# Gated feed-forward block on one core: the first of seven block products copied into the second's PSUM pair, and the second product moved behind that copy

## The chip, the core and the metric

The kernel runs on one core of a Trainium2 chip. The metric is device time in microseconds (us) of one execution; the kernel before has a median of 394.66 us over three runs (394.34 to 394.94). Engine names here: TensorE (PE in the rows), its weight loads (PEld), VectorE (DVE), ScalarE (ACT), GpSimd (POOL), and SP, which issues DMAs. SBUF is the on-chip memory of the engines, PSUM the accumulators that TensorE writes: eight banks, used here as four pairs `pair0` to `pair3` of 128 x 1024 float32.

## The reference

Four batches of 512 rows with 512 columns pass a gated cross-attention block and then a gated feed-forward block with ternary weights. Only the second part is touched:

```python
def ternary_quant(w):
    scale = jnp.mean(jnp.abs(w)) + EPS
    return jnp.clip(jnp.round(w / scale), -1.0, 1.0) * scale
...
x = x + jnp.tanh(g_xattn[0]) * xattn(layernorm(x), ctx_1024, Wq, bq, Wk, bk)
xn = layernorm(x)
hidden = jax.nn.silu(xn @ wu.T) * (xn @ wg.T)        # (4, 512, 512) x (2048, 512)
x = x + jnp.tanh(g_ffn[0]) * (hidden @ wd.T)         # (4, 512, 2048) x (512, 2048)
```

## The kernel before, in words

**Attention (0 to 92 us of the profile).** It is left as it is.

**Up and gate products, units 0 to 15.** A unit `n` makes a block of `hidden` for 256 of the 2048 expert columns and half of the 2048 rows; units 0 to 7 take the first half, 8 to 15 the second. The product is a 2 x 2 block product in seven block products (Winograd's form of Strassen's scheme). Activations are split into a high and a low float16 part, so one block product is 8 matmuls of 512 columns: up and gate (two banks of a PSUM pair), two inner chunks, high and low (`product`, L924 and L926). The seven are numbered 1 to 7 and accumulate in PSUM where the scheme allows it (`start=False`): 1, 6, 7 and 4 run on `ps_c[n % 2]` (`pair0` or `pair3`, by turns), 5 and 3 on `ps_z` (`pair2`), and 2 alone on `ps_y` (`pair1`).

The four result blocks are called by their place. ScalarE copies partial sums out between the products and VectorE adds the rest:

- "11" = product 1 + product 2: `copy_1` (ScalarE, L1373) copies `ps_c` after product 1 to SBUF, `add_11` (VectorE, L1789) adds `ps_y` to that.
- "12": `copy_u2` (L1383) copies `ps_c` after product 6, `add_12` (L1794) adds `ps_z`.
- "22": `copy_5` (L1395) copies `ps_z` after product 5, `add_22` (L1799) adds `ps_c` after product 7; product 4 waits for it.
- "21" = `ps_c` after product 4, read in place.

Each block then passes `silu` (ScalarE, L1344), `make_h` (VectorE, L1804: silu times gate) and the split into high and low parts (`high_h` on ScalarE, L1357, `low_h` on VectorE, L1809). Product 1 of unit n+2 overwrites the pair that `make_h(n, "21")` reads.

**Down product.** Units 0 to 5 go through it as plain matmuls, in `down_half(n)` within units 3 to 8 (32 matmuls of 512 columns, L1000). The rest is a second seven-product scheme, `final(g, j, t, ...)` (L1052, 256 columns), whose pieces 1, 5, 6, 3, 7, 2, 4 are strewn between the block products of units 9 and 10 (`between_two`, two tiles at once, 8 matmuls) and 12 to 15 (`between`, one tile, 8 matmuls). Their results lie in the `ps_c` pair that the unit itself does not use; VectorE adds them to the output (`final_evict`, L1855), and product 1 of the next unit (10, 11, 13, 14, 15) waits for the last of these seven additions, the one of piece 4 (`s_ef`), because it overwrites that pair. Each piece also waits for an earlier piece's addition where both use the same bank.

**Side work.** In units 0 to 7 ScalarE also rounds and signs the ternary weights of later units and of the down matrix (`round_unit` L1209, `sign_unit` L1215, `round_down` L1410, `sign_down` L1418). From unit 6 on GpSimd forms sums S1 to S4 of the result blocks for the second scheme, and ScalarE and VectorE split them (`high_s` L1363, `low_s` L1814).

Each engine's order is written out by hand in its own block; only semaphores tie them. On TensorE the order before is, for units 0 to 7, 6, 3, (`down_half`), 7, then 1, 2, 5 of the next unit, then 4. The lines that the change touches:

```python
            def product2(n):
                if n == 0:
                    pe.wait_ge(s_exp, NG)
                else:
                    pe.wait_ge(s_c["11"], n)
                product(n, 2, ps_y, A12, "B21", True)
...
                act.activation(cb(n, "11"), ps_c[n % 2][:, :], ACT.Copy).then_inc(s_cp1, 1)
...
                dve.tensor_tensor(cb(n, "11"), ps_y[:, :], cb(n, "11"), ALU.add).then_inc(s_c["11"], 1)
```

Of the kernel before, what the change touches and what calls it, by code (L numbers as in the profile page):

```python
# [6 lines left out]
def gated_block_kernel(nc, x, xT, first, ctxT, wqkT, wugT, wdT, x1_dram, out):  # L7
# [25 lines left out]
    NN = 2 * NU  # L33
# [12 lines left out]
    with stack:  # L46
# [55 lines left out]
        cbuf = {"11": [xf[:, 0:1024]], "12": [xf[:, 1024:2048]],  # L102
# [39 lines left out]
        s_c = {c: sem(f"s_c{c}") for c in ("11", "12", "22")}  # L142
# [624 lines left out]
        def _(pe):  # L767
# [265 lines left out]
            product2(G0 + 1)  # L1033
            product4(G0)
            product5(G0 + 1)
# [66 lines left out]
            product2(n + 1)  # L1102
            product4(n)
            product1(n + 1)
            product5(n + 1)
            for n in range(G1, NN):
# [8 lines left out]
                else:  # L1115
                    product2(n)
# [3 lines left out]
                    between(n, 5)  # L1120
                    product6(n)
# [17 lines left out]
            pe.wait_ge(s_c["11"], NN)  # L1139
# [27 lines left out]
        def _(act):  # L1167
# [163 lines left out]
            def silu(n, c):  # L1331
                if c == "21":
# [5 lines left out]
                    src = ps_c[n % 2][:, 0:512]  # L1338
                else:
# [80 lines left out]
            sign_part(2, 0)  # L1420
            act.wait_ge(s_t4, 1)
            copy_1(0)
# [4 lines left out]
            copy_u2(0)  # L1427
            silu(0, "11")
            for n in range(G0 + 1):
                down = n >= 3  # L1430
                if n > 0:
                    silu(n - 1, "21")
                    copy_u2(n)
# [4 lines left out]
                if n > 0:  # L1438
                    high_h(n - 1, "21")
# [62 lines left out]
                copy_1(n + 1)  # L1502
# [5 lines left out]
                if n == 1:  # L1508
                    copy_5(n + 1)
                    silu(n + 1, "11")  # L1510
                else:
                    silu(n + 1, "11")
                    copy_5(n + 1)
            for n in (G0 + 1, G0 + 2):
# [7 lines left out]
                else:  # L1522
                    high_s(n - 1, "S1")
                    high_h(n - 1, "21")
                    high_s(n - 1, "S2")
                    copy_5(n)
                    copy_1(n)
# [638 lines left out]
```

## Time and profile before

| what | value |
|---|---|
| median of 3 runs | 394.66 us (394.34 to 394.94) |
| span of the profiled execution, first to last instruction | 393.2 us |
| TensorE busy | 388.2 us, 99% of the span |
| VectorE busy | 330.2 us, 84% |
| ScalarE busy | 269.8 us, 69% |
| GpSimd busy | 183.9 us, 47% |
| `add_11`, 16 times | 19.5 us of VectorE |
| `copy_1`, 16 times | 16.2 us of ScalarE |

The profiled execution is one of its own; of it the page gives the span, and what lies around the span is not in it. The median of the runs is 1.46 us above that span. Matmuls are pipelined: a row's duration (0.38 us for 512 columns) is longer than the distance to the next start (0.21 to 0.22 us), and the ends are modelled, so a wait of TensorE shows as idle time only beyond that overlap of some 0.16 us.

### The profile page before, as it was taken

How to read it: one execution, taken by the hardware profiler on the slowest of the kernel's cores; microseconds unless marked ns; L12 is line 12 of the kernel's file. 1: busy time of each engine (PE TensorE's matmuls, PEld its weight loads, DVE VectorE, ACT ScalarE, POOL GpSimd, SP SyncE). 2: the span in 40 equal slices, each digit the busy share in tenths (PEclk: the TensorE clock that was granted, in tenths of full speed). 3: DMA queues.
4: the chain of work that ended last, by engine and by line, in shares of the span. 5: the costliest groups of instructions: out<-in, count | busy, mean ns of one | idle time of the engine just before them, and what ended most of it. 6: DMA issues, size and time to landing. Idle time of an engine off the chain costs nothing.

```text
span 393.2 us, 6214 instructions
## 1 busy us (share of the span) xinstructions
PE 388.2 (99%) x2000; PEld 219.3 (56%) x2000; DVE 330.2 (84%) x501; ACT 269.8 (69%) x366; POOL 183.9 (47%) x199
## 2 busy tenths in 40 slices
PE   8999999999999999999999999999999999999997
PEld 6676775554444444444444444556545665656886
DVE  0778897988799975789888979999999989798974
ACT  3887988899777786869897982856287566564400
POOL 0498727767845031403169462643639447261000
DMA  8999977799600030020029470006230000000014
GB/s 287 404 402 407 408 232 184 176 261 183 160 2 0 1 108 0 13 96 0 2 60 190 86 148 2 0 1 214 78 139 0 2 1 2 0 2 1 2 61 154
DMA packets 44048, 43.91 MB, mean 112 GB/s; under 512 B 30833, under 2 KB 33009, under 8 KB 42993
## 3 DMA queue, kind: packets, MB, share of 16 engines
q1 hardware_dynamic: 44016, 43.53, 36.3%
q8 instruction: 16, 0.26, 0.3%
q14 instruction: 16, 0.12, 0.1%
HBM read 29.89 MB, written 6.29 MB: 92 GB/s over the span
## 4 chain that ended last, share of the span: by engine, by line
PE 84%; DVE 6%; ACT 4%; issue 4%; DMA 1%; POOL 1%; DVEq 0%; ACTq 0%; POOLq 0%
PE pair L924 20%; PE pair L926 20%; PE pair L1052 14%; PE pair L1000 8%; PE pair L815 7%; PE pair L838 6%; PE pair L788 4%; PE pair L772 3%; PE pair L799 2%; DVE x_sb L1855 1%; DVE xf L1804 1%; DMA xf<-in_first 1%; PE pair L853 1%; DVE sh L1814 1%; ACT xf L1395 1%
## 5 line engine op out<-in xcount | busy, mean ns | idle before, releaser
L924 PE MATMUL pair<-xb_hi,w_sb 128*128 128x512 f16 x448 | 169.8, 379 | 0.9 <-DVE xf L1799 0.5
L926 PE MATMUL pair<-xb_lo,w_sb 128*128 128x512 f16 x448 | 169.8, 379 | 0.0
L924 PEld LDWEIGHTS pair<-xb_hi,w_sb 128*128 128x128 fp8e4 x448 | 43.8, 98 | 54.0 <-DVE xf L1799 1.3
L926 PEld LDWEIGHTS pair<-xb_lo,w_sb 128*128 128x128 fp8e4 x448 | 43.8, 98 | 49.5 <-issue 0.3
L1344 ACT ACTIVATE xf<-xf,small 128x512 f32<-128x512 f32 x48 | 34.5, 720 | 43.5 <-DVE xf L1799 23.6
L1804 DVE SCALAR_TENSOR_TENSOR xf<-xf,small 128x512 f32<-128x512 f32 x48 | 41.7, 870 | 8.5 <-ACT xf L1344 8.4
L1855 DVE SCALAR_TENSOR_TENSOR x_sb<-pair,small,x_sb 128x256 f32<-128x256 f32 (+1 forms) x85 | 37.4, 472 | 6.3 <-PE pair L1052 5.8
L1000 PE MATMUL pair<-x_sb,sh 128*128 128x512 bf16 x192 | 42.4, 379 | 0.0
L626 POOL TENSOR_TENSOR w_sb<-w_sb 128x512 fp8e4<-128x512 fp8e4 x8 | 8.8, 1101 | 55.1 <-ACT w_sb L1215 55.1
L1000 PEld LDWEIGHTS pair<-x_sb,sh 128*128 128x128 f16 x192 | 18.8, 98 | 22.6 <-DVE x_sb L1839 0.2
L1809 DVE TENSOR_TENSOR sh<-xf,sh 128x512 f16<-128x512 f32 x34 | 30.6, 906 | 0.9 <-ACT sh L1357 0.8
L1357 ACT ACTIVATE sh<-xf 128x512 f16<-128x512 f32 x34 | 20.9, 623 | 13.0 <-DVE xf L1804 12.3
L815 PE MATMUL pair<-sh,xt_sb 128*128 128x512 f32 (+2 forms) x80 | 28.6, 509 | 0.0
L1794 DVE TENSOR_TENSOR xf<-pair,xf 128x1024 f32<-128x1024 f32 x16 | 19.5, 1221 | 5.5 <-PE pair L926 5.4
L1789 DVE TENSOR_TENSOR xf<-pair,xf 128x1024 f32<-128x1024 f32 x16 | 19.5, 1220 | 3.8 <-issue 2.2
L713 POOL TENSOR_TENSOR xf<-xf 128x512 f32<-128x512 f32 x7 | 9.6, 1369 | 27.9 <-DVE xf L1804 27.9
L1373 ACT ACTIVATE xf<-pair 128x1024 f32<-128x1024 f32 x16 | 16.2, 1014 | 8.9 <-PE pair L926 6.4
L1799 DVE TENSOR_TENSOR xf<-pair,xf 128x1024 f32<-128x1024 f32 x16 | 19.5, 1218 | 2.3 <-PE pair L926 2.3
L1839 DVE SCALAR_TENSOR_TENSOR x_sb<-pair,small,x_sb 128x512 f32<-128x512 f32 x24 | 17.7, 745 | 3.9 <-PE pair L1000 3.9
L815 PEld LDWEIGHTS pair<-sh,xt_sb 128*128 128x128 f32 x80 | 13.9, 190 | 12.6 <-issue 10.5
L1383 ACT ACTIVATE xf<-pair 128x1024 f32<-128x1024 f32 x16 | 16.3, 1020 | 5.5 <-PE pair L926 5.3
L1209 ACT ACTIVATE w_sb<-w_sb,small 128x1024 f32<-128x1024 f32 x16 | 18.9, 1228 | 0.0
(207 smaller groups left out, 769.2 us busy)
## 6 DMA issues: line engine op xcount, KB each, us to landing
w_sb<-in_wugT SPq DMA_DIRECT2D x8, 1024.0 KB, 14.9
x_sb<-in_x SPq DMA_DIRECT2D x4, 1024.0 KB, 12.8
xf<-in_wdT SPq DMA_DIRECT2D x4, 1024.0 KB, 7.5
xt_sb<-in_wdT SPq DMA_DIRECT2D x4, 1024.0 KB, 4.9
xt_sb<-in_xT SPq DMA_DIRECT2D x12, 256.0 KB, 5.8
x_dram<-x_sb SPq DMA_DIRECT2D x8, 256.0 KB, 3.5
out<-x_sb SPq DMA_DIRECT2D x8, 256.0 KB, 4.2
x_sb<-x_dram SPq DMA_DIRECT2D x4, 512.0 KB, 3.9
```

The source lines that it names most:

```text
L815: last = pe.matmul(ps_x[i % 2][:, lo:hi], xt_tile(b, i)[:, k, :], at[:, k, lo:hi], start=(k == 0), stop=(k == KD - 1))
L838: last = pe.matmul(mix_bank(j)[:, i * 256:(i + 1) * 256], left[:, i, k * P:(k + 1) * P], right[:, k, :], start=j in (1, 5, 2) and i == 0 a ...
L924: pe.matmul(dst[:, m * 512:(m + 1) * 512], w[:, o:o + P], hi[:, k], start=start and k == 0, stop=False, skip_group_check=not start)
L926: last = pe.matmul(dst[:, m * 512:(m + 1) * 512], w[:, o:o + P], lo[:, k], start=False, stop=k == 1, skip_group_check=not start)
L1000: ins = pe.matmul(dst, h_part(n, c, lo)[:, i * P:(i + 1) * P], t_d[:, e * DM + lo_col:e * DM + hi_col], start=first and n == units[0] and ...
L1052: ins = pe.matmul(fin_bank(g, j, t), hidden(u, c, lo, min(t, NT - 1)), cols, start=first and u == units[0] and lo == 0 and not (side and t ...
L1344: act.activation(cb(n, c)[:, 0:512], src, ACT.Silu, scale=su[:, :]).then_inc(s_silu[c], 1)
L1357: act.activation(part(n, c, 0), shaped(n, c, cb(n, c)[:, 0:512]), ACT.Copy).then_inc(s_hi[c], 1)
L1789: dve.tensor_tensor(cb(n, "11"), ps_y[:, :], cb(n, "11"), ALU.add).then_inc(s_c["11"], 1)
L1804: dve.scalar_tensor_tensor(cb(n, c)[:, 0:512], cb(n, c)[:, 0:512], kap[:, :], gate, ALU.mult, ALU.mult).then_inc(s_mul[c], 1)
L1809: dve.tensor_tensor(part(n, c, 1), shaped(n, c, cb(n, c)[:, 0:512]), part(n, c, 0), ALU.subtract)\
L1855: dve.scalar_tensor_tensor(fin_rows(g, j, t), fin_bank(g, j, t), c_out[:, :], fin_rows(g, j, t), ALU.mult, ALU.add).then_inc(s_ef, 1)
```

## The change: what it does

`copy_1` writes into `ps_y` instead of SBUF. Product 2 now waits for that copy (`s_cp1`) and accumulates onto it (`start=False`), so "11" is complete in PSUM. `add_11` is gone. `silu(n, "11")` reads `ps_y` and writes SBUF, `make_h(n, "11")` takes its gate from `ps_y`, and `copy_1` waits until the unit before has passed that `make_h` (`s_mul["11"]`), since it overwrites `ps_y`. The orders on the three engines are rewritten. The core of the diff:

```diff
-                if n == 0:
-                    pe.wait_ge(s_exp, NG)
-                else:
-                    pe.wait_ge(s_c["11"], n)
-                product(n, 2, ps_y, A12, "B21", True)
+                pe.wait_ge(s_cp1, n + 1)
+                product(n, 2, ps_y, A12, "B21", False)
...
                 product1(n + 1)
+                product5(n + 1)
                 product2(n + 1)
-                product5(n + 1)
                 product4(n)
...
-            product2(G0 + 1)
+            product5(G0 + 1)
             product4(G0)
-            product5(G0 + 1)
             product1(G0 + 1)
...
                 between_two(n, 1)
                 between_two(n, 5)
+                product2(n)
                 product6(n)
...
                 between_two(n, 2)
-                product4(n)
-                between_two(n, 4)
-                product2(n + 1)
                 if n == G0 + 1:
+                    product4(n)
+                    between_two(n, 4)
                     product5(n + 1)
                     product1(n + 1)
                 else:
+                    between_two(n, 4)
+                    product5(n + 1)
                     product1(n + 1)
-                    product5(n + 1)
+                    product4(n)
+                    product2(n + 1)
...
-                    product2(n)
                     product5(n)
                     product1(n)
                     between(n, 1)
                     between(n, 5)
+                    product2(n)
                     product6(n)
...
+                elif c == "11":
+                    act.wait_ge(s_p[2], n + 1)
+                    if n == 0:
+                        act.wait_ge(s_tl, t_done(0, "T2"))
+                    else:
+                        act.wait_ge(s_lo["11"], n)
+                    if n > GB:
+                        act.wait_ge(s_sh["S3"], n - GB)
+                    src = ps_y[:, 0:512]
...
             def copy_1(n):
                 act.wait_ge(s_p[1], n + 1)
                 if n == 0:
-                    act.wait_ge(s_tl, t_done(0, "T2"))
-                else:
-                    act.wait_ge(s_lo["11"], n)
-                if n > GB:
-                    act.wait_ge(s_sh["S3"], n - GB)
-                act.activation(cb(n, "11"), ps_c[n % 2][:, :], ACT.Copy).then_inc(s_cp1, 1)
+                    act.wait_ge(s_exp, NG)
+                else:
+                    act.wait_ge(s_mul["11"], n)
+                act.activation(ps_y[:, :], ps_c[n % 2][:, :], ACT.Copy).then_inc(s_cp1, 1)
...
-            def add_11(n):
-                dve.wait_ge(s_p[2], n + 1)
-                hold(dve, s_cp1, n + 1)
-                dve.tensor_tensor(cb(n, "11"), ps_y[:, :], cb(n, "11"), ALU.add).then_inc(s_c["11"], 1)
...
-                gate = ps_c[n % 2][:, 512:1024] if c == "21" else cb(n, c)[:, 512:1024]
+                gate = {"21": ps_c[n % 2], "11": ps_y}.get(c, cb(n, c))[:, 512:1024]
```

In the rows below, a row with `pair1` as its output on TensorE is product 2, `pair2` product 5 or 3, `pair0` and `pair3` products 1, 6, 7, 4; the words in brackets are the semaphores waited for.

ScalarE between units 0 and 1, before: two weight roundings, `silu(0, "22")`, `copy_1(1)`, two splits, `silu(1, "11")`, `copy_5(1)`.

```order
L1209 ACTIVATE w_sb<-w_sb,small 128x1024 [waits s_inv]
L1209 ACTIVATE w_sb<-w_sb,small 128x1024
L1344 ACTIVATE xf<-xf,small 128x512 [waits s_coef,s_c22]
L1373 ACTIVATE xf<-pair3 128x1024 [waits s_lo11,s_p1]
L1357 ACTIVATE sh<-xf 128x512 [waits s_mul12]
L1357 ACTIVATE sh<-xf 128x512 [waits s_mul22]
L1344 ACTIVATE xf<-xf,small 128x512 [waits s_c11]
L1395 ACTIVATE xf<-pair2 128x1024 [waits s_tl,s_p5]
```

ScalarE in the same place now:

```order
L1208 ACTIVATE w_sb<-w_sb,small 128x1024 [waits s_inv]
L1208 ACTIVATE w_sb<-w_sb,small 128x1024
L1379 ACTIVATE pair1<-pair3 128x1024 [waits s_mul11,s_p1]
L1352 ACTIVATE xf<-xf,small 128x512 [waits s_coef,s_c22]
L1401 ACTIVATE xf<-pair2 128x1024 [waits s_tl,s_p5]
L1365 ACTIVATE sh<-xf 128x512 [waits s_mul12]
L1365 ACTIVATE sh<-xf 128x512 [waits s_mul22]
L1352 ACTIVATE xf<-pair1,small 128x512 [waits s_lo11,s_p2]
```

`copy_1` moved ahead of `silu(0, "22")` but stays behind the two roundings; `copy_5` moved ahead of the two splits.

TensorE at the end of unit 12, before: the last piece 4, product 2 of unit 13 (8 rows), then product 5; product 1 follows after 8 rows of product 5.

```order
L1052 MATMUL pair3<-w_sb,sh 128x256 [waits s_tw,s_lo22,s_ef]
L1052 MATMUL pair3<-w_sb,sh 128x256 x7
L924 MATMUL pair1<-xb_hi,w_sb 128x512 [waits s_c11]
L926 MATMUL pair1<-xb_lo,w_sb 128x512
L924 MATMUL pair1<-xb_hi,w_sb 128x512
L926 MATMUL pair1<-xb_lo,w_sb 128x512
L924 MATMUL pair1<-xb_hi,w_sb 128x512
L926 MATMUL pair1<-xb_lo,w_sb 128x512
L924 MATMUL pair1<-xb_hi,w_sb 128x512
L926 MATMUL pair1<-xb_lo,w_sb 128x512
L924 MATMUL pair2<-xb_hi,w_sb 128x512 [waits s_c12]
```

TensorE in the same place now:

```order
L1048 MATMUL pair3<-w_sb,sh 128x256 [waits s_tw,s_lo22,s_ef]
L1048 MATMUL pair3<-w_sb,sh 128x256 x7
L924 MATMUL pair2<-xb_hi,w_sb 128x512 [waits s_c12]
L926 MATMUL pair2<-xb_lo,w_sb 128x512
L924 MATMUL pair2<-xb_hi,w_sb 128x512
L926 MATMUL pair2<-xb_lo,w_sb 128x512
L924 MATMUL pair2<-xb_hi,w_sb 128x512
L926 MATMUL pair2<-xb_lo,w_sb 128x512
L924 MATMUL pair2<-xb_hi,w_sb 128x512
L926 MATMUL pair2<-xb_lo,w_sb 128x512
L924 MATMUL pair3<-xb_hi,w_sb 128x512 [waits s_ef,s_ev,s_mul21]
```

Between piece 4 and product 1 (the row that waits for `s_ef`) stood two products; now one stands there. The eight matmuls of product 2 come after the next pieces 1 and 5. The same holds in units 9, 10, 14 and 15.

VectorE at the start of unit 13, now: the addition of piece 4 of unit 12, three splits, two additions of pieces, `make_h(13, "11")` with its gate from `pair1`, `add_12`. Before, `add_11` (`L1789 TENSOR_TENSOR xf<-pair1,xf 128x1024`) stood behind the three splits.

```order
L1800 SCALAR_TENSOR_TENSOR c21<-c21,small,pair3 128x512 [waits s_silu21]
L1851 SCALAR_TENSOR_TENSOR x_sb<-pair0,small,x_sb 128x256 [waits s_fin]
L1810 TENSOR_TENSOR w_sb<-xf,w_sb 128x512 [waits s_shiS1]
L1805 TENSOR_TENSOR w_sb<-c21,w_sb 128x512 [waits s_hi21]
L1810 TENSOR_TENSOR w_sb<-xf,w_sb 128x512 [waits s_shiS2]
L1851 SCALAR_TENSOR_TENSOR x_sb<-pair3,small,x_sb 128x256 [waits s_fin,s_shift] x2
L1800 SCALAR_TENSOR_TENSOR xf<-xf,small,pair1 128x512 [waits s_silu11]
L1790 TENSOR_TENSOR xf<-pair2,xf 128x1024 [waits s_p3,s_cu2]
```

The addition of piece 4 is where it was; what was taken out stood behind it.

## Rows read from the trace of the kernel before

**Rows 1.** Stretches: time, busy time of PE, PEld, DVE, ACT, POOL, clock, DMA

```profile
92.00:230.00 138.00, 138.00 (x640) 62.29 (x639) 116.22 (x139) 110.76 (x128) 62.85 (x55) 1.00 0.27 66
230.00:300.00 70.00, 68.81 (x372) 35.62 (x370) 65.57 (x91) 41.10 (x62) 35.47 (x24) 1.00 0.23 71
300.00:366.00 66.00, 66.00 (x419) 40.72 (x418) 58.00 (x77) 39.33 (x59) 31.03 (x21) 1.00 0.00 1
```

**Rows 2.** Costliest groups of the page: the removed addition (busy, mean ns, idle before)

```profile
L1789 DVE TENSOR_TENSOR xf<-pair,xf 128x1024 f32<-128x1024 f32 x16 | 19.5, 1220 | 3.8 <-issue 2.2
```

**Rows 3.** Timeline, unit 10 (start, duration, engine): additions of piece 7; product 4, piece 4

```profile
278.32 0.86 DVE L1855 SCALAR_TENSOR_TENSOR x_sb<-pair,small,x_sb 128x256 f32<-128x256 f32 x2
...
277.84 0.38 PE L924 MATMUL pair<-xb_hi,w_sb 128*128 128x512 f16 x1
...
279.57 1.04 PE L1052 MATMUL pair<-w_sb,sh 128*128 128x256 bf16 x8
```

**Rows 4.** Timeline, unit 9: end of product 1, make_h(8,"21"), piece 1

```profile
247.45 0.75 DVE L1804 SCALAR_TENSOR_TENSOR c<-c,small,pair 128x512 f32<-128x512 f32 x1 [0.28 <-ACT c L1344]
...
247.69 0.38 PE L926 MATMUL pair<-xb_lo,w_sb 128*128 128x512 f16 x1
248.26 1.05 PE L1052 MATMUL pair<-x_sb,sh 128*128 128x256 bf16 x8 [0.18 <-DVE c L1804]
```

**Rows 5.** Timeline, units 9 and 10: add_22(9), additions of piece 4; products 4, 1

```profile
258.11 1.21 DVE L1799 TENSOR_TENSOR xf<-pair,xf 128x1024 f32<-128x1024 f32 x1
...
264.56 0.86 DVE L1855 SCALAR_TENSOR_TENSOR x_sb<-pair,small,x_sb 128x256 f32<-128x256 f32 x2
...
259.38 0.39 PE L924 MATMUL pair<-xb_hi,w_sb 128*128 128x512 f16 x1 [0.53 <-DVE xf L1799]
...
265.69 0.38 PE L924 MATMUL pair<-xb_hi,w_sb 128*128 128x512 f16 x1
```

**Rows 6.** Timeline, unit 12: product 6's start

```profile
298.19 0.39 PE L924 MATMUL pair<-xb_hi,w_sb 128*128 128x512 f16 x1 [0.26 <-ACT xf L1373]
```

**Rows 7.** Timeline, units 7 and 8: sign_down(3), third product's start, product 6 to 3

```profile
222.89 1.99 ACT L1418 ACTIVATE x_sb<-xt_sb,small 128x2048 bf16<-128x2048 f32 x1
225.15 0.38 PE L924 MATMUL pair<-xb_hi,w_sb 128*128 128x512 f16 x1
...
230.11 0.38 PE L926 MATMUL pair<-xb_lo,w_sb 128*128 128x512 f16 x1
230.63 0.39 PE L924 MATMUL pair<-xb_hi,w_sb 128*128 128x512 f16 x1
```

**Rows 8.** One line of the kernel, copy_1: shortest, median, longest in ns

```profile
L1373 ACT ACTIVATE xf<-pair x16: 1000/1018/1027, 94.5 to 353.0; 128x1024 f32<-128x1024 f32 x16
```

**Rows 9.** Timeline: last matmul of unit 3's product 6, and its copy

```profile
135.08 0.38 PE L926 MATMUL pair<-xb_lo,w_sb 128*128 128x512 f16 x1
135.49 1.02 ACT L1383 ACTIVATE xf<-pair 128x1024 f32<-128x1024 f32 x1 [0.61 <-PE pair L926]
```

**Rows 10.** Timeline, units 0 and 1: weight rounding and sign; third product's start

```profile
104.19 2.36 ACT L1209 ACTIVATE w_sb<-w_sb,small 128x1024 f32<-128x1024 f32 x2
105.91 0.38 PE L924 MATMUL pair<-xb_hi,w_sb 128*128 128x512 f16 x1
...
116.64 1.99 ACT L1215 ACTIVATE w_sb<-w_sb,small 128x2048 fp8e4<-128x2048 f32 x1
```

**Rows 11.** Timeline, units 12 and 13: add_22(12), addition of piece 4; product 1

```profile
306.46 1.22 DVE L1799 TENSOR_TENSOR xf<-pair,xf 128x1024 f32<-128x1024 f32 x1
...
313.87 0.47 DVE L1855 SCALAR_TENSOR_TENSOR x_sb<-pair,small,x_sb 128x256 f32<-128x256 f32 x1
...
314.68 0.38 PE L924 MATMUL pair<-xb_hi,w_sb 128*128 128x512 f16 x1
```

**Rows 12.** Timeline, units 13 and 14: addition of piece 4; product 1

```profile
330.86 0.47 DVE L1855 SCALAR_TENSOR_TENSOR x_sb<-pair,small,x_sb 128x256 f32<-128x256 f32 x1
...
332.88 0.38 PE L924 MATMUL pair<-xb_hi,w_sb 128*128 128x512 f16 x1
```

More of the change, by code:

```diff
@@ L1420, in _ @@
             sign_part(2, 0)
+            copy_1(0)
             act.wait_ge(s_t4, 1)
-            copy_1(0)
             act.wait_ge(s_tl, t_done(0, "T3"))
@@ L1426, in _ @@
             copy_5(0)
-            copy_u2(0)
-            silu(0, "11")
             for n in range(G0 + 1):
                 down = n >= 3
+                silu(n, "11")
                 if n > 0:
                     silu(n - 1, "21")
-                    copy_u2(n)
+                copy_u2(n)
+                if n > 0:
+                    high_h(n - 1, "21")
                 if n == 7:
@@ L1491, in _ @@
                     sign_down(3)
+                if n < G0:
+                    copy_1(n + 1)
                 silu(n, "22")
@@ L1501, in _ @@
                     break
-                copy_1(n + 1)
+                copy_5(n + 1)
                 if not down:
@@ L1523, in _ @@
                     high_s(n - 1, "S1")
+                    copy_5(n)
                     high_h(n - 1, "21")
+                    copy_1(n)
                     high_s(n - 1, "S2")
-                    copy_5(n)
-                    copy_1(n)
                 high_s(n - 1, "S4")
@@ L1540, in _ @@
             n = G1 - 1
+            copy_5(n)
+            copy_1(n)
+            high_h(n - 1, "22")
             silu(n - 1, "21")
-            copy_1(n)
-            copy_5(n)
             silu(n, "11")
-            high_h(n - 1, "22")
+            high_s(n - 1, "S1")
             copy_u2(n)
-            high_s(n - 1, "S1")
+            high_h(n - 1, "21")
             high_s(n - 1, "S2")
-            high_h(n - 1, "21")
             silu(n, "12")
@@ L1552, in _ @@
             high_s(n - 1, "S4")
+            copy_1(n + 1)
             silu(n, "22")
@@ L1555, in _ @@
             shift(3, 0)
+            copy_5(n + 1)
             silu(n, "21")
-            copy_1(n + 1)
             high_s(n, "S1")
-            copy_5(n + 1)
             high_s(n, "S2")
+            silu(n + 1, "11")
             high_s(n, "S3")
-            silu(n + 1, "11")
+            high_h(n, "21")
             high_s(n, "S4")
-            high_h(n, "21")
             for n in range(G1, NN):
@@ L1879, in _ @@
                 down = 3 <= n
+                make_h(n, "11")
                 if n > 2:
@@ L1883, in _ @@
                     ternary_down(3)
-                make_h(n, "11")
                 add_12(n)
@@ L1913, in _ @@
                 make_h(n, "22")
-                add_11(n + 1)
                 if not down:
@@ L1950, in _ @@
             make_h(n, "22")
-            add_11(n + 1)
             low_t(NU, "T4", xf_half(2, 1))
@@ L2002, in _ @@
             low_s(n - 1, "S2")
[L2003 removed]
             evict_two(n, 1)
+            evict_two(n, 5)
             make_h(n, "11")
[L2006 removed]
             add_12(n)
@@ L2013, in _ @@
             evict_two(n, 7)
+            evict_two(n, 2)
             make_h(n, "22")
-            evict_two(n, 2)
+            evict_two(n, 4)
             n = G1 - 1
+            weights_1(0)
+            low_h(n - 1, "22")
             make_h(n - 1, "21")
-            evict_two(n - 1, 4)
-            weights_1(0)
-            add_11(n)
+            make_h(n, "11")
             weights_t2(0)
-            make_h(n, "11")
-            low_h(n - 1, "22")
             weights_t4(0)
@@ L2033, in _ @@
             make_h(n, "21")
-            add_11(n + 1)
             low_s(n, "S1")
@@ L2043, in _ @@
                     low_s(n - 1, "S2")
-                    add_11(n)
-                final_evict(0, 1, t)
-                if n == G1:
+                    final_evict(0, 1, t)
+                    final_evict(0, 5, t)
+                    make_h(n, "11")
+                else:
+                    make_h(n, "11")
                     low_s(n - 1, "S2")
-                make_h(n, "11")
-                if n > G1:
-                    final_evict(0, 5, t)
+                    final_evict(0, 1, t)
                 add_12(n)
@@ L2086, in _ @@
             low_s(n - 1, "S2")
-            add_11(n)
             final_evict(0, 1, 3)
-            make_h(n, "11")
             weights_1(1)
             final_evict(0, 5, 3)
+            make_h(n, "11")
             add_12(n)
```

25 lines of the change are left out of this document (7 added, 18 removed).

## Prediction

> **What bounds the kernel now.** I read the busy time by stretches first. From 92 to 230 us and from 300 to 366 us TensorE is busy for the whole of each stretch at clock 1.00; between 230 and 300 us it lacks 1.19 us [rows 1]. VectorE is the next, with 65.57 of 70 us in that middle stretch. So TensorE sets the time in units 0 to 15, and since the change adds and removes no matmul, only TensorE's waits can move the time: those that are there can go, and new ones can come. 19.5 us of VectorE's work go with `add_11` [rows 2], but none of that is worth anything by itself.
>
> Then I looked in the timeline for the places where TensorE waits, and for how long each release came before the matmul that it releases. One block product lasts 279.57 - 277.84 = 1.73 us [rows 3], so a matmul of 512 columns starts 0.216 us after the last. A wait shows as idle less some 0.16 us (0.38 us of row, 0.216 us of pace). The waits of before are then 248.26 - 247.69 - 0.22 = 0.35 us before piece 1 of unit 9 [rows 4], 0.53 + 0.16 = 0.69 us before product 4 of unit 9 [rows 5], 0.26 + 0.16 = 0.42 us before product 6 of unit 12 [rows 6] and 230.63 - 230.11 - 0.22 = 0.30 us before product 3 of unit 8 [rows 7]: 1.76 us in all. That is nearly all that can be gained.
>
> **The change, part by part.**
>
> *The chain product 1, copy, product 2.* Between product 1 and product 2 one other block of work now stands: product 5, or pieces 1 and 5 from unit 9 on. A copy takes 1.018 us [rows 8]. Where ScalarE is free it starts at once: unit 3's `copy_u2` runs 135.49 to 136.51 after product 6, whose last matmul starts at 135.08, and a product after the next one would start at 135.08 + 0.22 + 1.73 = 137.03 [rows 9]. The copy is then hidden with 0.5 us to spare. Where ScalarE is late by more than that, TensorE waits.
>
> - Unit 0 to 1: `copy_1(1)` stands behind two roundings that end at 104.19 + 2.36 = 106.55 [rows 10]. They follow `silu(0, "12")`, whose input VectorE made behind `add_11(0)`; without that 1.22 us [rows 2] I take them to end at 105.33 and the copy at 106.35. Product 2 would start where the third product stood, at 105.91 [rows 10]: 0.44 us of waiting (0 if ScalarE gains more, 1.66 us if it gains nothing).
> - Unit 1 to 2: a sign pass ends at 116.64 + 1.99 = 118.63 [rows 10], 117.41 with the same gain, the copy at 118.43; the place of product 2 is seven products after 105.91, at 118.02, and 118.46 with the wait before it. Nothing.
> - Units 2 to 6: by the timeline ScalarE has ended its side work in time for the copy. Nothing.
> - Unit 7 to 8: `sign_down(3)` ends a run of side work at 222.89 + 1.99 = 224.88, the copy at 225.90; product 2's place is 225.15 [rows 7]: 0.75 us (0 to 0.75). In return `copy_5(8)` comes earlier, ahead of two instructions that stood before it, and the 0.30 us before product 3 go.
>
> A copy into PSUM is not in this trace. All copies of this size here end in SBUF, and I take their 1.018 us, the nearest row. The Trainium skill, Perfetto Trace Analysis, section Optimizing Scalar/DVE Operations, gives ScalarE a fixed cost of about 51 ns on PSUM against about 93 ns on SBUF. By an estimate from that page each of the two waits above would be some 0.04 us shorter; no run here shows it. The other end is a copy of twice the length, a rival below.
>
> *Product 2 leaves the gap between piece 4 and the next product 1.* In units 9, 10, 13, 14 and 15 product 2 was work that TensorE did while VectorE caught up. The release itself stays where it is, so what it had to spare is set against the 1.73 us by which TensorE now arrives earlier.
>
> - Piece 1 of unit 9 waits for `make_h(8, "21")`, done at 247.45 + 0.75 = 248.20; it waits 0.35 us already [rows 4], so the whole 1.73 us become waiting. What makes it late (two shifts and a split on ScalarE after `silu(8, "22")`) stays in its order.
> - Product 1 of unit 10 waits for the additions of piece 4, done at 264.56 + 0.86 = 265.42, and starts at 265.69 [rows 5]: 0.27 us to spare, 1.46 us lost. VectorE is behind here, which shows in the 0.69 us before product 4 [rows 5]; that chain starts at `add_22(9)`, 258.11, and a queue without `add_11(9)` reaches it earlier. If the whole 0.69 us goes, 0.77 us are left; I take 1.1 us, the middle.
> - Unit 10 has product 4 moved as well: piece 4 now follows piece 2 at once. It needs the additions of piece 7, done at 278.32 + 0.86 = 279.18, and starts at 279.57 [rows 3]: 0.39 us to spare, 1.34 us lost.
> - Product 1 of unit 13: the addition of piece 4 is done at 313.87 + 0.47 = 314.34, the product starts at 314.68 [rows 11]: 0.34 us to spare, 1.39 us lost. VectorE works from `add_22(12)` at 306.46 to that addition without a pause, and `add_11` is not among this work: it stood behind it. So the relief doesn't reach this release.
> - Product 1 of unit 14: 330.86 + 0.47 = 331.33 against 332.88 [rows 12]: 1.55 us to spare, 0.18 us lost. Unit 15 repeats the pattern: 0.18 us.
>
> *What product 2 covers in its new place.* It now stands before product 6, which waits for the same copy. Only unit 12 waited there, 0.42 us [rows 6], and this goes, as two more products stand between now. VectorE's free 1.22 us a unit lie after the additions of piece 4 and become idle time.
>
> *Small parts.* `silu` and `make_h` of "11" read PSUM instead of SBUF, as those of "21" did before (0.75 us for `make_h` [rows 4]): nothing, off the path. No DMA is added, and none is issued past another.
>
> **Sum.** 0.44 + 0.75 - 0.30 + 1.73 + 1.1 + 1.34 + 1.39 + 2 x 0.18 - 0.42 = 6.4 us on the profiled span of 393.2 us: 399.6 us. The median stands 1.46 us above that span, and I leave that as it is: **401.1 us**. With every low end together (no waits for copies, 0.77 for unit 10) it is 4.9 us, with every high end (1.66 for unit 1, 1.46 for unit 10, the 0.30 and 0.42 not regained) 8.7 us: 399.5 to 403.4 us.
>
> **The rivals.**
>
> *VectorE's relief reaches the releases (faster).* VectorE is busy for 94% of the middle stretch [rows 1], and four of the five late releases are its work. If it holds a backlog from unit to unit, `add_11` gone makes each release earlier. From 1.73 us earlier on no new wait is left; then the 1.76 us of old waits can go too, the copies being hidden: 392.9 us. For it speaks `add_22(9)`, which started late [rows 5]; against it `add_22(12)` and the work behind it, which follow product 7 and not `add_11` [rows 11]. The Trainium skill, Perfetto Trace Analysis, section Optimization Strategies, says that when the matmul engine idles for other engines, those that block the critical path are to be relieved. By that rule this change relieves the right engine; the trace agrees that VectorE blocks (0.53 us of idle put down to it [rows 5]), but not that the removed work lies in the blocking chain. 7 in 100.
>
> *Half of it.* Releases 0.61 us earlier (half an addition): unit 9 loses 1.12, unit 10 0.85 - 0.69 and 0.73, unit 13 0.78, units 14 and 15 nothing; with 0.89 for the copies and -0.42, 3.3 us: 397.9 us. 15 in 100. A whole addition earlier everywhere leaves 0.8 us, 395.5 us, on the edge of what can be told. 5 in 100.
>
> *The copy is dear.* If a copy from PSUM into PSUM takes twice as long, it misses its place by 0.5 us in the six unit changes where it was hidden and by 1 us more in the other two, some 5 us on top: 406 us. Nothing in the trace speaks for it. 4 in 100.
>
> *The waits are exchanged one for one.* If what product 2 covers in its new place is as much as what it uncovers, 394.7 us; the rows show only one wait of 0.42 us there. 3 in 100.
>
> **How the numbers follow.** The forecast has the rest, 66 in 100. The range takes it in from its high end, 403.4 us, down past the half relief, to 396.6 us; 19 in 100 are left out. A measurement of this kernel can tell 0.2%, 0.8 us, from no change. Slower by more than that: forecast, half relief, dear copy and 2 of the 5 for the whole addition, 0.87. Within it: the other 3 and the exchange, 0.06. Faster: 0.07.
>
> **What the profile after would show.** Right: TensorE idle before piece 1 of unit 9 for about 1.9 us (released by `make_h` of "21"), before product 1 of units 10 and 13 and before piece 4 of unit 10 for more than 1 us each (released by the additions on VectorE); idle of some 0.3 to 0.7 us before product 2 of units 1 and 8, released by `copy_1`; none before product 6 of unit 12; VectorE about 19 us less busy, TensorE as busy as before. Wrong: the stretch from 230 to 300 us as full as before, which would mean that the releases moved with VectorE's relief; or copies far from 1.0 us.

## The result, and the profile after

The changed kernel takes 402.2 us (median of four runs, 401.8 to 403.18) against 394.5 us for the kernel before in the same job: 1.0198 times as long, 95% interval 1.0184 to 1.0212, or +7.7 us. The forecast was 401.1 us in a range of 396.6 to 403.4, slower with a chance of 0.87.

The profiled execution has a span of 401.4 us, 8.2 us above that of before; the other three have 400.0 to 400.4. The page's row of busy times:

```profile
PE 389.4 (97%) x2000; PEld 219.2 (55%) x2000; DVE 312.4 (78%) x485; ACT 269.3 (67%) x366; POOL 181.2 (45%) x199
```

TensorE is as busy as before (389.4 us against 388.2), VectorE is 17.8 us less busy, and the span is longer. So time went into waits of TensorE. The stretches of [rows 1], in the profile after (time, busy time of PE, PEld, DVE, ACT, POOL, clock, DMA):

```profile
92.00:230.00 138.00, 137.00 (x633) 61.47 (x632) 105.89 (x130) 110.79 (x129) 61.28 (x53) 1.00 0.26 65
230.00:300.00 70.00, 65.30 (x356) 34.17 (x354) 56.66 (x81) 37.75 (x57) 30.93 (x24) 1.00 0.24 74
300.00:366.00 66.00, 63.62 (x385) 37.17 (x383) 52.77 (x68) 40.74 (x61) 34.57 (x24) 1.00 0.00 1
```

The granted clock is 1.00, the upper of its two levels, in all three stretches. From 92 to 230 us TensorE lacks 1.00 us and from 300 us on 2.38, both full before; between them it lacks 4.70 us (1.19 before). VectorE got its relief: 56.66 us against 65.57 in the middle stretch. By itself that did not make the kernel faster.

All places after 92 us where TensorE idles, from the timeline (start, duration, engine, line, in the brackets the idle time and what ended it):

```profile
106.48 0.39 PE L924 MATMUL pair<-xb_hi,w_sb 128*128 128x512 f16 x1 [0.16 <-ACT pair L1379]
119.00 0.39 PE L924 MATMUL pair<-xb_hi,w_sb 128*128 128x512 f16 x1 [0.26 <-ACT pair L1379]
226.81 0.39 PE L924 MATMUL pair<-xb_hi,w_sb 128*128 128x512 f16 x1 [0.58 <-ACT pair L1379]
249.49 0.28 PE L1048 MATMUL pair<-x_sb,sh 128*128 128x256 bf16 x1 [1.79 <-DVE c L1800]
261.97 0.39 PE L924 MATMUL pair<-xb_hi,w_sb 128*128 128x512 f16 x1 [0.16 <-DVE xf L1795]
268.16 0.38 PE L924 MATMUL pair<-xb_hi,w_sb 128*128 128x512 f16 x1 [1.44 <-DVE x_sb L1851]
283.43 0.28 PE L1048 MATMUL pair<-w_sb,sh 128*128 128x256 bf16 x1 [1.24 <-DVE x_sb L1851]
309.51 0.28 PE L1048 MATMUL pair<-w_sb,xt_sb 128*128 128x256 bf16 x1 [0.83 <-DVE x_sb L1851]
320.44 0.38 PE L924 MATMUL pair<-xb_hi,w_sb 128*128 128x512 f16 x1 [1.22 <-DVE x_sb L1851]
338.97 0.38 PE L924 MATMUL pair<-xb_hi,w_sb 128*128 128x512 f16 x1 [0.16 <-DVE x_sb L1851]
357.49 0.38 PE L924 MATMUL pair<-xb_hi,w_sb 128*128 128x512 f16 x1 [0.17 <-DVE x_sb L1851]
```

The first three are product 2 of units 1, 2 and 8, released by `copy_1` (now L1379). Then come piece 1 of unit 9 (released by `make_h`, now L1800), product 4 of unit 9 (`add_22`, L1795), product 1 of unit 10, piece 4 of unit 10, piece 6 of unit 12, and product 1 of units 13, 14 and 15, these six released by additions of pieces (L1851). Each wait is the idle time and some 0.16 us more, as in the prediction. Product 3 of unit 8 and product 6 of unit 12 wait no longer. Place by place, in us:

| place | forecast | wait after, less wait before |
|---|---|---|
| product 2 of unit 1 | 0.44 | 0.32 |
| product 2 of unit 2 | 0 | 0.42 |
| product 2 and product 3 of unit 8 | 0.75 - 0.30 | 0.74 - 0.30 |
| piece 1 of unit 9 | 1.73 | 1.95 - 0.35 = 1.60 |
| product 4 of unit 9 and product 1 of unit 10 | 1.1 | 0.32 - 0.69 + 1.60 = 1.23 |
| piece 4 of unit 10 | 1.34 | 1.40 |
| product 6 of unit 12 | -0.42 | -0.42 |
| piece 6 of unit 12 | not in it | 0.99 |
| product 1 of unit 13 | 1.39 | 1.38 |
| product 1 of units 14 and 15 | 0.36 | 0.32 + 0.33 |
| sum | 6.4 | 8.0 |

With product 1 of unit 0 starting 0.24 us later (92.34 against 92.10), that is the 8.2 us between the two spans. The profiled execution is the slowest of the four, so its difference is larger than the 7.7 us of the medians. Where product 1 of unit 0 starts differs from one profiled execution to the next, although the attention ahead of it is the same in all of them: 90.84 to 92.45 us in the eleven profiles of this case. For small differences the profiles are therefore compared below from that start to the start of the last four matmuls: 297.97 us in the kernel before, 305.87 in the changed one, 7.90 us more.

### The profile page after: what moved, and what is told of

It reads as the page before. It is cut to its first block, busy times and chain, and to the rows that moved or that the text cites. A ratio compares the mean times of both kernels' runs of the same rounds, so it can differ in the third digit from the quotient of the medians.

```text
span 401.4 us, 6198 instructions
## 1 busy us (share of the span) xinstructions
PE 389.4 (97%) x2000; PEld 219.2 (55%) x2000; DVE 312.4 (78%) x485; ACT 269.3 (67%) x366; POOL 181.2 (45%) x199
## 4 chain that ended last, share of the span: by engine, by line
PE 77%; DVE 9%; ACT 7%; issue 6%; DMA 1%; POOL 0%; DVEq 0%; ACTq 0%; POOLq 0%
PE pair L924 17%; PE pair L926 17%; PE pair L1048 13%; PE pair L997 8%; PE pair L815 7%; PE pair L838 6%; PE pair L788 3%; PE pair L772 3%; PE pair L799 2%; DVE sh L1805 2%; DVE x_sb L1851 2%; DVE xf L1800 1%; DVE xf L1790 1%; PE pair L853 1%; DMA xf<-in_first 1%
## 5 line engine op out<-in xcount | busy, mean ns | idle before, releaser
L1352 ACT ACTIVATE xf<-xf,small 128x512 f32<-128x512 f32 x32 | 23.0, 718 | 35.6 <-DVE xf L1795 19.8
L1851 DVE SCALAR_TENSOR_TENSOR x_sb<-pair,small,x_sb 128x256 f32<-128x256 f32 (+1 forms) x85 | 37.1, 472 | 5.7 <-PE pair L1048 5.2
L1800 DVE SCALAR_TENSOR_TENSOR xf<-xf,small 128x512 f32<-128x512 f32 x32 | 28.0, 874 | 11.9 <-ACT xf L1352 11.9
L1805 DVE TENSOR_TENSOR sh<-xf,sh 128x512 f16<-128x512 f32 x34 | 31.5, 932 | 6.3 <-ACT sh L1365 6.1
L626 POOL TENSOR_TENSOR w_sb<-w_sb 128x512 fp8e4<-128x512 fp8e4 x8 | 9.8, 1225 | 55.5 <-ACT w_sb L1214 55.5
L1790 DVE TENSOR_TENSOR xf<-pair,xf 128x1024 f32<-128x1024 f32 x16 | 19.6, 1222 | 18.8 <-PE pair L926 18.8
L1365 ACT ACTIVATE sh<-xf 128x512 f16<-128x512 f32 x34 | 21.1, 622 | 9.5 <-DVE xf L1800 8.8
L1389 ACT ACTIVATE xf<-pair 128x1024 f32<-128x1024 f32 x16 | 16.4, 1023 | 13.8 <-PE pair L926 13.8
L1795 DVE TENSOR_TENSOR xf<-pair,xf 128x1024 f32<-128x1024 f32 x16 | 19.5, 1219 | 3.5 <-PE pair L926 3.5
L1379 ACT ACTIVATE pair<-pair 128x1024 f32<-128x1024 f32 x16 | 16.1, 1007 | 8.4 <-PE pair L926 8.4
L1048 PE MATMUL pair<-x_sb,sh 128*128 128x256 bf16 (+1 forms) x132 | 17.4, 269 | 1.8 <-DVE c L1800 1.8
```

Source lines behind the costliest of these rows:

```text
L1048: ins = pe.matmul(fin_bank(g, j, t), hidden(u, c, lo, min(t, NT - 1)), cols, start=first and u == units[0] and lo == 0 and not (side and t ...
L1352: act.activation(cb(n, c)[:, 0:512], src, ACT.Silu, scale=su[:, :]).then_inc(s_silu[c], 1)
L1365: act.activation(part(n, c, 0), shaped(n, c, cb(n, c)[:, 0:512]), ACT.Copy).then_inc(s_hi[c], 1)
L1790: dve.tensor_tensor(cb(n, "12"), ps_z[:, :], cb(n, "12"), ALU.add).then_inc(s_c["12"], 1)
L1800: dve.scalar_tensor_tensor(cb(n, c)[:, 0:512], cb(n, c)[:, 0:512], kap[:, :], gate, ALU.mult, ALU.mult).then_inc(s_mul[c], 1)
L1805: dve.tensor_tensor(part(n, c, 1), shaped(n, c, cb(n, c)[:, 0:512]), part(n, c, 0), ALU.subtract)\
```

## The experiments

The theory: the time is TensorE's waits, each made by the order of a queue on ScalarE or VectorE, which product 2 used to cover. Against it stand the rivals that the accumulation itself is dear, and that VectorE simply lacks the time.

**Units 0 to 8 alone (low_only).** Units 9 to 15 keep the old product 2 and `add_11`.

```diff
-                pe.wait_ge(s_cp1, n + 1)
-                product(n, 2, ps_y, A12, "B21", False)
+                if n <= G0:
+                    pe.wait_ge(s_cp1, n + 1)
...
+                product(n, 2, ps_y, A12, "B21", n > G0)
```

> Units 0 to 8 as changed, units 9 to 15 as before. Theory (the time is TensorE's waits, place by place): of the changed kernel's waits only those before product 2 of units 1, 2 and 8 stay (0.32, 0.42 and 0.74 us), the 0.30 us before product 3 of unit 8 are gone: +1.2 us, 395.7 us, ratio 1.003; product 1 of units 10 and 13 start without a wait. Rival (accumulating onto a copy costs something in every unit): 9 of 16 units carry 9/16 of 7.7 us, +4.3 us, 398.8 us, ratio 1.011.

Measured: 395.15 us, ratio 1.0013 (1.0004 to 1.0023), that is +0.5 us. Its trace has the three waits before product 2 (of these, 0.58 us of idle at unit 8), and none before product 1 of units 10 and 13. The nine changed units cost far less than the rival's 4.3 us, and by the time even less than the 1.2 us of the theory. First row of product 1 of unit 0 and the last four matmuls, in the kernel before and then here:

```profile
92.10 0.38 PE L924 MATMUL pair<-xb_hi,w_sb 128*128 128x512 f16 x1
390.07 0.39 PE L1052 MATMUL pair<-x_sb,sh 128*128 128x128 bf16 x4
```

```profile
91.75 0.38 PE L924 MATMUL pair<-xb_hi,w_sb 128*128 128x512 f16 x1
390.75 0.39 PE L1054 MATMUL pair<-x_sb,sh 128*128 128x128 bf16 x4
```

Between them lie 297.97 and 299.00 us: 1.03 us more, near the theory, and in these two executions what is missing lies ahead of the units, where the attention ended 0.35 us earlier. By difference, most of the 7.7 us lies in units 9 to 15.

**The copy ahead of side work (copy_first).** `copy_1(1)` goes between the two halves of the weight rounding, `copy_1(2)` ahead of `sign_unit(3)`, `copy_1(8)` ahead of `sign_down(3)`.

```diff
                 for m in range(2):
+                    if u == 3 and m == 1:
+                        copy_1(1)
...
-                if n == 1:
-                    sign_unit(3)
...
+                if 0 < n < G0:
+                    copy_1(n + 1)
                 if n == 7:
                     sign_down(3)
-                if n < G0:
-                    copy_1(n + 1)
                 silu(n, "22")
+                if n == 1:
+                    sign_unit(3)
```

> The changed kernel with the first product's copy ahead of the second weight rounding (unit 1), the sign pass of unit 3 (unit 2) and the last sign pass of the down matrix (unit 8) on ScalarE. Theory (the copy is late because it queues behind side work): the three waits before product 2 go, 0.32 + 0.42 + 0.74 = 1.5 us less than the changed kernel's 402.2: 400.7 us, ratio 1.016. Rival (a copy into PSUM and the accumulation onto it are late by themselves): the waits stay and the time is 402.2 us, ratio 1.020.

Measured: 401.12 us, ratio 1.0166 (1.0151 to 1.018), 1.1 us less than the changed kernel, of 1.5 expected; from product 1 of unit 0 to the last matmuls its profile has 304.47 us, 1.40 less. The waits of TensorE in its profile (engine and line, waited for, total, times, longest):

```profile
PE pair L924 <- DVE x_sb L1853: 3.0, 4, 1.4
PE pair L1048 <- DVE x_sb L1853: 2.1, 2, 1.2
PE pair L1048 <- DVE c L1802: 1.8, 1, 1.8
PE pair L849 <- POOL early L536: 1.0, 1, 1.0
PE pair L924 <- DVE xf L1797: 0.2, 1, 0.2
```

No wait for a copy is left, and all the others stand as they were. The copy and the accumulation are not late by themselves; the queue ahead of the copy is.

**The addition of piece 4 ahead in units 12 to 14 (piece4_add_first).**

```diff
                     make_h(n - 1, "21")
-                    final_evict(0, 4, t - 1)
...
                 final_evict(0, 2, t)
+                final_evict(0, 4, t)
                 low_h(n, "22")
...
-            final_evict(0, 4, 2)
```

> The changed kernel with one move on VectorE in units 12 to 14: the addition of piece 4 ahead of a split (1.36 us in unit 12) and of make_h of block 21 (0.73 us). Theory (product 1 of units 13 to 15 waits for VectorE's queue, which product 2 used to cover): the addition comes 2.0 us earlier, and the waits of 1.37, 0.32 and 0.32 us before these products go: 2.0 us less than 402.2, 400.2 us, ratio 1.015. Rival (the addition is late because piece 4 itself is late, or the displaced work is needed as soon): the waits stay or come back before piece 1 of the next unit, 402.2 us, ratio 1.020.

Measured: 401.52 us, ratio 1.0178 (1.016 to 1.0197): less than half of the forecast 2.0 us. The three waits before product 1 are gone, but three new ones stand one step later, before product 2 of units 13 to 15. In the timeline of unit 14, first ScalarE, then TensorE:

```profile
337.41 0.63 ACT L1365 ACTIVATE w_sb<-c 128x512 f16<-128x512 f32 x1 [1.81 <-DVE c L1800]
337.95 0.61 ACT L1371 ACTIVATE w_sb<-xf 128x512 f16<-128x512 f32 x1
338.46 1.00 ACT L1401 ACTIVATE xf<-pair 128x1024 f32<-128x1024 f32 x1
339.37 1.01 ACT L1379 ACTIVATE pair<-pair 128x1024 f32<-128x1024 f32 x1
...
340.44 0.39 PE L924 MATMUL pair<-xb_hi,w_sb 128*128 128x512 f16 x1 [0.45 <-ACT pair L1379]
```

The `make_h` of block 21 that gave way on VectorE is awaited by a split on ScalarE (`high_h`, L1365, 1.81 us idle), and behind this in the queue stand `copy_5` and `copy_1`. The three waits that went made up 2.03 us, the three that came 1.64: the move itself gave 0.4 us. The rest of what the profile gained (305.09 us from product 1 of unit 0 to the last matmuls, 0.78 less) is the wait of 0.42 us before product 2 of unit 2, which this execution does not have. So the theory held for product 1 and the second half of the rival for the rest: the displaced work was due soon after, over one more engine.

**The order without the accumulation (order_only).** All three engines in the changed order; the copy goes to SBUF, product 2 starts its own sum, and `add_11` is back, ahead of `make_h` of block 11 or where it stood.

```diff
-                pe.wait_ge(s_cp1, n + 1)
-                product(n, 2, ps_y, A12, "B21", False)
+                if n == 0:
+                    pe.wait_ge(s_exp, NG)
+                else:
+                    pe.wait_ge(s_c["11"], n)
+                product(n, 2, ps_y, A12, "B21", True)
...
                 make_h(n, "22")
+                add_11(n + 1)
```

> The orders of the changed kernel with the arithmetic of before: the copy goes to SBUF, product 2 starts its own sum and VectorE adds the two again, 16 additions of 1.22 us. Theory (the order on TensorE makes the waits, the accumulation itself costs nothing): the waits of units 9 to 15 stay, those for the copies before product 2 (1.5 us) go, and where VectorE is late each addition can add up to 1.2 us: 400.7 to 405, about 403 us, ratio 1.021. Rival (the accumulation onto the copy is what costs): near the kernel before, 394.5 to 396 us, ratio 1.00.

Measured: 409.77 us (408.56 to 411.1), ratio 1.0384 (1.0357 to 1.0411): above the whole range that was expected. The waits of its TensorE:

```profile
PE pair L1051 <- DVE c L1801: 3.9, 2, 2.0
PE pair L924 <- DVE x_sb L1852: 3.0, 4, 1.4
PE pair L1051 <- DVE x_sb L1852: 2.5, 2, 1.2
PE pair L1000 <- DVE x_sb L1836: 2.0, 1, 2.0
PE pair L1000 <- DVE c L1801: 1.2, 2, 0.8
```

The four waits before product 1 (3.0 us) and the two before pieces (2.5 us here, 2.1 in the changed kernel) are those of the changed kernel. New are 3.2 us in the down product of units 3 to 8 (L1000) and a second wait before a piece 1. So the order costs 15 us with the addition in it (14.07 in the profile, from product 1 of unit 0 to the last matmuls), and 7.7 us with the accumulation in its place. Where `add_11` was put is mine; another place might cost less. The rival, that the accumulation is what costs, is out. The fourth combination, the accumulation in the order of before, was not run.

**The queues of units 8 to 10 (queue_mid).** Work that TensorE waits for goes ahead of work that it does not wait for.

```diff
                 if n == G0:
+                    silu(n, "21")
                     high_h(n, "22")
                     shift(1, 0)
...
             low_h(n, "11")
+            make_h(n, "21")
             low_h(n, "22")
...
             add_22(n)
-            low_h(n, "11")
             evict_two(n, 7)
             make_h(n, "22")
             evict_two(n, 2)
+            low_h(n, "11")
+            evict_two(n, 4)
...
-            add_22(n)
             low_h(n, "11")
             evict_two(n, 7)
             evict_two(n, 2)
+            evict_two(n, 4)
+            add_22(n)
             make_h(n, "22")
-            evict_two(n, 4)
```

> The changed kernel with moves in the queues of VectorE and ScalarE in units 8 to 10 alone: silu and make_h of block 21 of unit 8 ahead of two shifts and two splits; in unit 9 the additions of pieces 7, 2 and 4 ahead of splits; in unit 10 the additions of pieces 7, 2 and 4 ahead of add_22. Theory (TensorE waits for work that is ready but queued behind work that is not due, which product 2 used to cover): the waits of 1.95, 0.33, 0.24, 1.60 and 1.40 us go but for some 0.3 us: 5.2 us less than 402.2, 397.0 us, ratio 1.006. Rival (VectorE is the bound of these units, so a move only puts off the wait): the displaced splits come late instead, and the time stays over 400 us, ratio over 1.014.

Measured: 399.25 us, ratio 1.0124 (1.0106 to 1.0143): -3.0 us of the 5.2 expected. The five waits shrink to about 0.4 us in all, but product 2 of unit 9 now shows 1.31 us of idle before it, released by its copy, and piece 6 of unit 12 1.25 us instead of 0.83. More than half of the theory; the rest moved on, most of it to ScalarE's queue.

**The addition of piece 1 ahead in unit 12 (piece1_add_first).** This undoes one line of the change.

```diff
-                    make_h(n, "11")
-                    low_s(n - 1, "S2")
                     final_evict(0, 1, t)
+                    low_s(n - 1, "S2")
+                    make_h(n, "11")
```

> The changed kernel with VectorE's order in unit 12 as it was: the addition of piece 1 ahead of the split of S2 and of make_h of block 11, where the change had put it behind both. Theory (the 1.01 us before piece 6 of unit 12, which the prediction did not have, come from this one move and nothing else): they go, and the waits behind them stay at 1.37, 0.32 and 0.32 us or get smaller: 1.0 us less than 402.2, 401.2 us, ratio 1.017. Rival (the sums of GpSimd that reach this place late are the cause, whatever VectorE's order): piece 6 waits as long, 402.2 us, ratio 1.020.

Measured: 401.55 us, ratio 1.0177 (1.016 to 1.0193), about 0.8 us less by the ratios, whose intervals overlap; from product 1 of unit 0 to the last matmuls the profile has 305.18 us, 0.69 less. On VectorE, in the changed kernel and then here (`make_h`, the split, the addition; here in the opposite order):

```profile
306.79 0.75 DVE L1800 SCALAR_TENSOR_TENSOR xf<-xf,small,pair 128x512 f32<-128x512 f32 x1 [0.80 <-ACT xf L1352]
307.45 1.60 DVE L1810 TENSOR_TENSOR t_sb<-xf,t_sb 128x512 f16<-128x512 f32 x1
308.98 0.47 DVE L1851 SCALAR_TENSOR_TENSOR x_sb<-pair,small,x_sb 128x256 f32<-128x256 f32 x1
```

```profile
304.68 0.48 DVE L1851 SCALAR_TENSOR_TENSOR x_sb<-pair,small,x_sb 128x256 f32<-128x256 f32 x1 [0.22 <-PE pair L1048]
305.08 1.06 DVE L1810 TENSOR_TENSOR t_sb<-xf,t_sb 128x512 f16<-128x512 f32 x1
306.07 0.74 DVE L1800 SCALAR_TENSOR_TENSOR xf<-xf,small,pair 128x512 f32<-128x512 f32 x1
```

The wait before piece 6 is gone. Product 1 of unit 13 waits 0.16 us more (1.38 of idle, 1.22 before), since TensorE reaches it sooner.

**All moves together (queue_all, queue_all_2).** The first puts the moves above together, with `copy_5` and `copy_1` of units 13 to 15 ahead of a split. The second adds four moves on ScalarE, shown against the first:

```diff
                     shift(1, 0)
+                    copy_1(n + 1)
                     shift(1, 1)
...
                     high_s(n - 1, "S1")
-                    copy_1(n)
                     high_h(n - 1, "21")
...
-            copy_5(n)
             copy_1(n)
+            copy_5(n)
...
             high_s(n, "S3")
-            high_h(n, "21")
+            copy_u2(n + 1)
             high_s(n, "S4")
+            high_h(n, "21")
...
                 if n == G1:
-                    copy_u2(n)
                     high_h(n - 1, "22")
```

> All moves together on the changed kernel: the copies ahead of side work (units 1, 2, 8), the moves of units 8 to 10, the addition of piece 1 of unit 12 ahead of a split and of make_h, the additions of piece 4 of units 12 to 14 ahead, and copy_5 and copy_1 of units 13 to 15 ahead of a split that waits for GpSimd. Theory (every wait of the changed kernel is an order on a queue, not a lack of engine time): 10.0 us of waits stand in its trace; with 0.5 to 1.5 us left over 393.2 us, ratio 0.9965. Rival (some of them are a lack of engine time on VectorE or GpSimd): over 395 us, ratio over 1.002.

> All moves of the run before that had them together, and four more on ScalarE for the waits that it still showed: copy_1 of unit 9 ahead of a shift and of a split that waits for GpSimd (1.48 us before product 2 of unit 9), copy_1 of unit 11 ahead of copy_5 (0.18 us), copy_u2 of unit 12 ahead of two splits (0.25 us before product 7 and 0.34 us before product 4). Theory (what is left is order on ScalarE again): 2.2 us less than 395.4, 393.2 us, ratio 0.9965, faster than the kernel before and even with its own moved version (393.6). Rival (the lack of time on VectorE and GpSimd returns elsewhere): over 394.5 us, ratio 1.000.

Measured: 395.38 us, ratio 1.0016 (1.0007 to 1.0025), then 393.49 us, ratio 0.9978 (0.9968 to 0.9989). The first ended 2.2 us above the 393.2 expected, mostly through one wait, 1.47 us (1.31 of idle) before product 2 of unit 9, whose copy stood behind two shifts, `copy_5` and a split. The second is faster than the kernel before by 0.9 us. The waits left in its TensorE, then its last two stretches:

```profile
PE pair L849 <- POOL early L536: 1.0, 1, 1.0
PE pair L924 <- DVE xf L1799: 0.5, 1, 0.5
PE pair L1048 <- DVE x_sb L1855: 0.2, 1, 0.2
```

```profile
230.00:300.00 70.00, 69.29 (x378) 36.51 (x378) 61.66 (x86) 40.58 (x61) 34.94 (x26) 1.00 0.23 72
300.00:366.00 66.00, 66.00 (x420) 40.82 (x418) 54.72 (x75) 38.70 (x59) 29.67 (x22) 1.00 0.00 1
```

VectorE does as much work as in the changed kernel (310.9 us busy against 312.4) and TensorE is nearly full: what the waits lacked was order, not engine time.

**The kernel before with moves of the same kind (before_moves).**

```diff
-            low_s(n - 1, "S2")
             make_h(n, "12")
             add_22(n)
-            low_h(n, "11")
             evict_two(n, 7)
+            low_s(n - 1, "S2")
+            low_h(n, "11")
```

and `silu(8, "21")`, `make_h(8, "21")` and `copy_5(8)` ahead, as above.

> The kernel before with moves of the same kind alone: silu and make_h of block 21 of unit 8 ahead, a split of unit 9 behind add_22, the additions of piece 7 ahead of it, copy_5 of unit 8 ahead of silu. Theory (the waits of before are of the same kind): 0.35 + 0.69 + 0.24 + 0.30 = 1.6 us go, 392.9 us, ratio 0.996. Rival (they move on to the next wait): 394.5 us, ratio 1.000.

Measured: 393.57 us, ratio 0.9973 (0.9962 to 0.9984), -1.0 us of the 1.6 expected: the wait before product 4 of unit 9 went from 0.53 to 0.27 us of idle, not to zero. It is level with the changed kernel after all its moves. So the change by itself brings nothing here that ordering the queues of before does not bring: outside the attention both have less than 1 us of waits of TensorE left.

## Why the prediction was right, point by point

**The bound.** "Only TensorE's waits can move the time" held: the waits, place by place, make the difference of the spans, and two kernels whose VectorE differs by 18 us (queue_all_2 and before_moves, 221.10 against 239.06 us from 92 to 366 us) come out level.

**Product 2 leaves the gap.** Four of five terms came within 0.15 us: 1.60 for 1.73, 1.23 for 1.1, 1.40 for 1.34 and 1.38 for 1.39; that for units 14 and 15 was 0.65 for 0.36. The method was to set the slack of each release against the 1.73 us by which TensorE arrives earlier. The releasers were named rightly too. The 1.1 us for units 9 and 10 was the middle between two bounds, 0.77 and 1.46, so that it came this near is partly luck. Of the signs that were named, the idle time before product 2 of unit 1 was smaller than said, 0.16 us against 0.3 to 0.7, and VectorE was 17.8 us less busy, not 19; the others came.

**The relief does not reach the releases.** In the changed kernel this stands: the wait before product 1 of unit 13 is what the old slack gave. But the relief was worth more than I said. I put `add_11` down as work whose loss only becomes idle time; order_only shows that with the addition back at the places chosen there the same order takes 409.8 us. The rival of the relief had the sign wrong, but VectorE's time does matter in the new order.

**The copy.** Hidden where ScalarE is free, as forecast, at 1.008 us (1.018 in [rows 8]). The gain on ScalarE before unit 1 was taken as one addition, 1.22 us; counted from product 1 of unit 0, which starts 0.24 us later here, the second rounding ends 1.27 us earlier (at 103.16 + 2.36 = 105.52 us, 106.55 before). Whether the addition alone did that is not shown, since other work was reordered too. For unit 2 I put the copy's end and product 2's place at 118.43 and 118.46, a gap of 0.03 us, and called it nothing; it was 0.42. The gain of 1.22 us was carried over to this unit, and the sign pass started only 0.83 us earlier (116.05 us, 116.64 before, and the 0.24); the shorter wait before product 2 of unit 1 added 0.12 us. In the profiles of low_only, queue_mid and piece1_add_first, with the same order there, the idle time is again 0.26 or 0.27 us, in that of piece4_add_first none. Where two ends meet within a few hundredths, the term is not zero but the spread of its parts.

**The step that was missing.** Piece 6 of unit 12, 0.99 us. The diff moves the addition of piece 1 behind `make_h` and a split; I followed the additions of pieces 4 and 7 through VectorE's new order and not this one. I looked where TensorE's order had changed, and this wait comes from VectorE's order: on TensorE, piece 6 still follows pieces 1 and 5 and product 3, and with VectorE's order undone the wait is gone. What made the place behind `make_h` so late is that `make_h` itself sits idle for 0.80 us, waiting for a `silu` whose product 2 the change had moved back. The 0.99 us are most of the 1.6 us by which the sum, 6.4 us, fell short of the 8.0 in the profile; the time itself fell short by 1.1 us.

**Chances.** The likeliest case came true, and the range held the time in its upper half, though not for its own reasons: its high end came from a larger wait in unit 1, a larger loss in unit 10 and old waits that stay, and none of these came. What filled it were piece 6, unit 2 and units 14 and 15.

## What to carry to other kernels

A product that fills a gap is worth what it covers: before moving it, set the slack of every release behind it against its length, and name the engine that is late. Then go through each reordered queue, not only that of the bounding engine, and ask of every instruction that moved back who waits for it. A release can often be pulled ahead in its queue, but follow the displaced work across engines too, since it may be due one step later.

## What the runs showed of the hardware

**VectorE beside GpSimd.** The split of 128 x 512 on VectorE takes between 0.68 us and more than twice that. Behind `make_h(11, "12")`, in the changed kernel, two splits take 1.64 and 1.75 us while GpSimd runs a split and a sum of its own; VectorE, then GpSimd:

```profile
298.51 1.64 DVE L1805 TENSOR_TENSOR sh<-c,sh 128x512 f16<-128x512 f32 x1
300.07 1.75 DVE L1805 TENSOR_TENSOR sh<-xf,sh 128x512 f16<-128x512 f32 x1
...
298.14 1.47 POOL L707 TENSOR_TENSOR t_sb<-xf,t_sb 128x512 f16<-128x512 f32 x1 [5.36 <-ACT t_sb L1371]
299.57 1.71 POOL L713 TENSOR_TENSOR xf<-xf 128x512 f32<-128x512 f32 x1
```

What I had not expected is what this does to `make_h` of block 11, whose gate moved from SBUF to PSUM. By line and form (shortest, median and longest in ns), with both inputs in SBUF and with the gate in PSUM:

```profile
L1800 DVE SCALAR_TENSOR_TENSOR xf<-xf,small x32: 735/744/2809, 104.7 to 374.1; 128x512 f32<-128x512 f32 x32
L1800 DVE SCALAR_TENSOR_TENSOR xf<-xf,small,pair x16: 731/744/749, 98.9 to 364.1; 128x512 f32<-128x512 f32 x16
```

All 16 with the gate in PSUM lie between 731 and 749 ns; before, with the gate in SBUF, four of the 16 took 1.02 to 1.65 us. Six of the 16 now run beside a TENSOR_TENSOR of GpSimd and take no longer for it; the 2.81 us of the other form stand beside one of 2.35 us. The Trainium skill, SBUF — State Buffer, section Who interferes with whom, says that a VectorE instruction with two SBUF inputs contends with a GpSimd instruction that reads SBUF, and that one with at most one SBUF input, outside the 2-port modes, does not. The trace agrees. The prediction had put this edit at nothing; what it is worth in time was not tried by itself.

**PSUM and SBUF as the copy's end.** From figures of the Trainium skill, Perfetto Trace Analysis, section Optimizing Scalar/DVE Operations, the prediction had worked out an estimate of 0.04 us less for a copy that ends in PSUM. The 16 copies measured 1.008 us against 1.018 [rows 8], 0.01 us less. The measurement decides, and neither matters to the sum. A difference of the estimated size appears where the source lies in PSUM: `silu` of the same size, always into SBUF, in the changed kernel (busy, mean ns):

```profile
L1352 ACT ACTIVATE xf<-xf,small 128x512 f32<-128x512 f32 x32 | 23.0, 718 | 35.6 <-DVE xf L1795 19.8 <-DVE xf L1790 15.8
L1352 ACT ACTIVATE xf<-pair,small 128x512 f32<-128x512 f32 x16 | 10.9, 680 | 7.7 <-PE pair L926 7.7
```
